# Separate semaphores for two groups of loads, an unrolled edge group, per-block waits in an expert's second layer, and first tokens over two queues

## The chip, the cores and the metric

The kernel runs on one core of one Trainium2 chip. The metric is the device time of one execution in microseconds; a profile of one further execution gives each engine's instructions with their times. Engines are named as in the profile: PE (TensorE; PEld is its weight load), DVE (VectorE), ACT (ScalarE), POOL (GpSimd), SP (SyncE, which here only issues transfers). SPq and ACTq are the sequencers of SP and ACT issuing transfers.

## The reference, cut to what matters

One layer on a graph of 3125 nodes (25 tiles of 128) with 256 features and 53125 edges sorted by `dst`:

```
xn = layernorm(x)
x  = x + gnn(xn, edges) + mix(xn)          # gnn: adjacency times features, two softmax layers; mix: linear attention
x  = x + moe(layernorm(x))                 # 8 experts, top 1, capacity 489 tokens
hmid = relu(einsum("ecd,edf->ecf", buf, w1) + b1)     # first layer of an expert, 256 -> 1024
ybuf = einsum("ecf,efd->ecd", hmid, w2) + b2          # second layer, 1024 -> 256
out  = x + gate * ybuf[token]
```

## The kernel before, in words

Each engine runs one instruction stream written out by hand; streams meet only at semaphores (`then_inc` raises one, `wait_ge` waits for a value), and an engine that waits holds everything behind it in its own stream.

**Start.** SP loads `dst`, DVE samples it, PE sums the samples, and DVE writes `base_i`: for each of the 25 tiles the place in the edge list at which its window begins. Meanwhile ACT issues the load of the first seven x tiles (`s_x[0]`) and of `wk`, `wv` (`s_kvw`), and then runs a small square root, with which the table of functions is loaded (L670). SP then runs over four groups of tiles, `GROUPS = ((0, 2), (2, 6), (6, 16), (16, 25))`. `window(g, j)` reads one number of `base_i` and issues three loads of 9 KB (`src`, `dst`, `edge_weight`), which raise `s_win[g]`. Group 0 is written out; the other three are loops on the sequencer (`sp.Fori`). After group 0 SP issues the rest of x (three loads and one short one, L454, L457) and the five weights `wo`, `wq`, `W0`, `W1`, `b1` (L461). After group 1 it issues eleven small constants (L451). The five and the eleven raise the same semaphore `s_w`, and whoever needs any of them waits for all 16.

**First stage, an iteration `it` for each tile.** ACT copies a turned tile (`turned`), casts a new group's windows (`cast(g)`, in the iteration before the group's first tile, L700 to L702), normalizes a tile, pairs (`paired`), squares (`squares`, after PE's `product`), and moves the records of the tile before out of PSUM (`kept`). DVE prepares a group (`prepare(g)`, L946 to L959), spreads a tile's edges (`spread`, L967, L969), takes statistics of x in `it < 3` and variances in `it == 2` and `scales(1)` in `it == 3`, slots the tile before (`slot(it - 1)`, L976, L979, L983) and, from `it == 2`, builds one-hot tiles (`hots`, L1023 to L1029). PE runs `product`, `ranks`, `slots` of the tile before, `build` from `it == 3` and the turn of the next tile. In `it == 1` it also runs `others()`, 15 transposes of `wo`, `W0`, `W1` and `b1` behind the wait for all of `s_w`; ACT moves them out in `others_out()`. POOL also waits for `s_w`, much later, after the attention matrix.

**Graph stages** (to about 947 us): adjacency blocks are built, applied and stored, then read back for two layers; this is not touched.

**Experts.** POOL scatters tokens into `xbuf_dram` (`s_disp`) and the rows to be kept into `rbuf_dram` (`s_dres`). PE runs `WARM` = 11 products of no use to cover the wait. SP issues `tokens(0, 0)` and `tokens(1, 1)`, four transfers of 128 KB each, then waits for `s_dres` and issues `kept_rows(0, 0)`, the output of x (`before(0, NT)`) and `kept_rows(1, 1)`. DVE transposes the tokens (`columns`, L1370), and for each expert PE runs

```
up(e):    8 blocks f, 2 matmuls each, into three PSUM banks           -> s_hid
ACT:      hidden(e): relu of block f into hmT[:, f, :]                -> s_hidv
down(e):  wait for s_hidv >= 8e + 8; 4 blocks of rows, each a sum over the 8 f   -> s_y
DVE:      yblock(e): 4 blocks of rows scaled and cleaned; POOL scatters them
```

A float32 matmul appears in the profile as two instructions.

Of the kernel before, what the change touches and what calls it, by code (L numbers as in the profile page):

```python
# [19 lines left out]
NT = 25  # L20
# [26 lines left out]
EPS = 1e-5  # L47
NWL = 16
XG = ((0, 7), (7, 13), (13, 19), (19, 25))
# [59 lines left out]
def graph_program(nc, a, out):  # L109
    ctx = ExitStack()  # L110
    with ctx:
# [227 lines left out]
        s_rstd = sem("s_rstd")  # L339
        s_w = sem("s_w")  # L340
        s_wt = sem("s_wt")
        s_wtc = sem("s_wtc")
# [83 lines left out]
        def _(sp):  # L426
# [10 lines left out]
            for g, (t0, t1) in enumerate(GROUPS):  # L437
                if g == 0:
                    for j in range(t0, t1):
                        window(g, j)  # L440
                else:
                    with sp.Fori(t0, t1) as j:
                        window(g, j)
                if g == 1:
                    for to, src in ((gate_w[:, :, :], half("L0_ffn_gate_w")), (bo_b[:, :], a["L0_mix_bo"].partition_broadcast(P)), (gb1_b[:, :], a["L0_gnn_b1"].partition_broadcast(P)),
                            (gate_b[:, :], a["L0_ffn_gate_b"].partition_broadcast(P)),
                            (gvb[:, 0, :], a["L0_mix_ln_v_g"].partition_broadcast(P)), (gvb[:, 1, :], a["L0_mix_ln_v_b"].partition_broadcast(P)),
                            (cols[:, 0:1], col("L0_gnn_b0")),
                            (cols[0:HD, 1:2], col("L0_mix_ln_k_g")), (cols[HD:P, 1:2], col("L0_mix_ln_k_g")),
                            (cols[0:HD, 2:3], col("L0_mix_ln_k_b")), (cols[HD:P, 2:3], col("L0_mix_ln_k_b"))):  # L450
                        sp.dma_start(to, src).then_inc(s_w, 16)  # L451
                for x in {0: (1, 2, 3)}.get(g, ()):
                    t0, last = XG[x][0], min(XG[x][1], NT - 1)
                    sp.dma_start(X1[:, t0:last, :], a["x"][t0 * P:last * P, :].rearrange("(j p) d -> p j d", p=P)).then_inc(s_x[x], 16)  # L454
                    if XG[x][1] == NT:
                        sp.wait_ge(s_zero, 1)
                        sp.dma_start(X1[0:LAST, last, :], a["x"][last * P:N, :]).then_inc(s_x[x], 16)  # L457
                if g == 0:
                    for to, src in ((wo_n, half("L0_mix_wo")), (wq_n, half("L0_mix_wq")), (W0_n, a["L0_gnn_W0"]),
                                    (W1_n, a["L0_gnn_W1"]), (b1_n, a["L0_ffn_b1"])):  # L460
                        sp.dma_start(to, src).then_inc(s_w, 16)  # L461
            sp.wait_ge(s_zero, 3)
# [48 lines left out]

            def tokens(e, s):
                blocks = xbuf_dram[ds(e * XS, XS), :].rearrange("(b j) (q f) -> q j b f", j=32, q=4)
                for q in range(4):
                    sp.dma_start(xbs[32 * q:32 * q + 32, s, :, :], blocks[q]).then_inc(s_tok[s], 16)
# [34 lines left out]
            sp.wait_ge(s_disp, 16 * NT)  # L550
            tokens(0, 0)
            tokens(1, 1)
            sp.wait_ge(s_dres, 16 * NT)
            kept_rows(0, 0)
            before(0, NT)
            kept_rows(1, 1)
# [107 lines left out]
        def _(act):  # L664
            half = lambda name: a[name].rearrange("(r p) n -> p r n", p=P)
            act.dma_start(X1[:, 0:XG[0][1], :], a["x"][0:XG[0][1] * P, :].rearrange("(j p) d -> p j d", p=P)).then_inc(s_x[0], 16)
            act.dma_start(wk_n, half("L0_mix_wk")).then_inc(s_kvw, 16)
            act.dma_start(wv_n, half("L0_mix_wv")).then_inc(s_kvw, 16)
            act.wait_ge(s_const, 2)
            nc.scalar.activation(rsum[:, 0, 0:1], ones_f[:, 0:1], ACT.Sqrt)  # L670
            act.wait_ge(s_const, 9)
# [87 lines left out]
            for it in range(NU + 3):  # L759
# [20 lines left out]
                if 0 <= u < NU:  # L780
                    evac(u)
                    if u - 1 in [strip_end(k) for k in range(NS)]:
                        strip_out(strip_of(u - 1))
                if it == 1:
                    others_out()
# [73 lines left out]
            def hidden(e):  # L859
                for f in range(8):  # L860
                    act.wait_ge(s_hid, 8 * e + f + 1)
                    if f == 0:
                        ge(act, s_y, 4 * e)
                    nc.scalar.activation(hmT[:, f, 0:CAPX], ps[:, 2 + f % 3, 0:CAPX], ACT.Relu, bias=b1T[:, f, e:e + 1]).then_inc(s_hidv, 1)  # L864
            for e in range(NE):
                hidden(e)
# [515 lines left out]
        def _(pe):  # L1382
# [15 lines left out]
            def others():  # L1398
                pe.wait_ge(s_w, 16 * NWL)
                for r in range(2):  # L1400
# [111 lines left out]
            for it in range(NU + 4):  # L1512
                if it < NT:
                    product(it)
                if it < NT:
                    ranks(it)
                if it == 1:
                    others()
# [204 lines left out]
            def down(e, s):  # L1723
                pe.wait_ge(s_hidv, 8 * e + 8)
                for c in range(4):
                    n = min(P, CAPX - c * P)
                    ge(pe, s_yv, 4 * e + c - 1)
                    o = ps[0:n, 5 + c % 2, 0:D]
                    for f in range(8):
                        last = nc.tensor.matmul(o, hmT[:, f, c * P:c * P + n], w2s[s][:, f, :], start=(f == 0), stop=(f == 7))  # L1730
                    last.then_inc(s_y, 1)
# [28 lines left out]
```

## Time and profile before

| what | us |
|---|---|
| median of 3 runs | 1199.76 |
| the runs | 1198.54 to 1200.06 |
| the profiled execution, its own time | 1197.42 |
| its span from first to last instruction | 1195.6 |
| PE busy | 1112.7 |
| DVE busy | 708.8 |
| ACT busy | 316.0 |
| mean granted TensorE clock | 0.976 of full speed |

The span is shorter than the time by 1.8 us that lie outside the instructions. A busy share is a mean over stages: PE is nearly always at work after the first 120 us, and far less before.

### The profile page before, as it was taken

How to read it: one execution, taken by the hardware profiler on the slowest of the kernel's cores; microseconds unless marked ns; L12 is line 12 of the kernel's file. 1: busy time of each engine (PE TensorE's matmuls, PEld its weight loads, DVE VectorE, ACT ScalarE, POOL GpSimd, SP SyncE). 2: the span in 40 equal slices, each digit the busy share in tenths (PEclk: the TensorE clock that was granted, in tenths of full speed). 3: DMA queues.
4: the chain of work that ended last, by engine and by line, in shares of the span. 5: the costliest groups of instructions: out<-in, count | busy, mean ns of one | idle time of the engine just before them, and what ended most of it. 6: DMA issues, size and time to landing. Idle time of an engine off the chain costs nothing.

```text
span 1195.6 us, 14060 instructions
## 1 busy us (share of the span) xinstructions
PE 1112.7 (93%) x4867; PEld 700.0 (59%) x4867; DVE 708.8 (59%) x1563; ACT 316.0 (26%) x1035; POOL 166.6 (14%) x206
## 2 busy tenths in 40 slices
PE   3589989999999999999998999999999699999995
PEld 2356656666666666666683444545558456666664
DVE  7798999998786877768740010204536334554443
ACT  3468767521212212112220111101112111222220
POOL 1013223301010100000000000000333511111111
PEclk9789989999999999999998999999999799999998
DMA  5111110122323333332238988787884564555510
GB/s 162 18 12 46 45 45 18 72 88 90 140 103 139 122 121 127 120 156 94 88 116 318 350 314 306 267 309 267 300 305 149 159 199 113 117 141 131 136 58 7
DMA packets 78724, 175.37 MB, mean 147 GB/s; under 512 B 33567, under 2 KB 62010, under 8 KB 66622
## 3 DMA queue, kind: packets, MB, share of 16 engines
q1 hardware_dynamic: 68462, 124.02, 32.8%
q10 hardware_dynamic: 6064, 42.40, 8.8%
q0 software_dynamic: 4128, 8.04, 1.9%
q8 instruction: 41, 0.67, 0.2%
q14 instruction: 29, 0.24, 0.1%
HBM read 113.82 MB, written 63.09 MB: 148 GB/s over the span
## 4 chain that ended last, share of the span: by engine, by line
PE 80%; DVE 9%; issue 3%; ACT 3%; another core or an unknown queue 2%; SPq 2%; DMA 1%; POOL 0%; POOLq 0%; DVEq 0%; ACTq 0%
PE ps L1481 20%; PE ps L1631 18%; PE ps L1464 11%; PE ps L1730 9%; PE ps L1719 9%; PE ps L1448 2%; PE ps L1507 2%; PE ps L1385 2%; PE ps L1434 2%; DVE W L983 1%; PE ps L1483 1%; PE ps L1733 1%; DVE RY L979 1%; ACT W L715 1%
## 5 line engine op out<-in xcount | busy, mean ns | idle before, releaser
L1481 PE MATMUL ps<-RING,XX 128*128 128x512 f32 x600 | 283.1, 594 | 0.3 <-ACT RING L743 0.3
L1631 PE MATMUL ps<-RING,RY 128*128 128x512 f32 (+2 forms) x750 | 277.5, 527 | 4.6 <-issue 4.6
L1631 PEld LDWEIGHTS ps<-RING,RY 128*128 128x128 f32 x750 | 134.0, 192 | 131.2 <-issue 129.1
L1464 PEld LDWEIGHTS ps<-RING 128*128 128x128 f32 x1250 | 163.7, 193 | 45.8 <-issue 44.7
L743 ACT COPY RING<-ps 128x512 f32<-128x512 f32 (+1 forms) x157 | 91.6, 584 | 317.0 <-PE ps L1464 300.7
L1464 PE MATMUL ps<-RING 128*128 128x128 f32 x1250 | 171.1, 278 | 0.5 <-ACT RING L733 0.5
L1481 PEld LDWEIGHTS ps<-RING,XX 128*128 128x128 f32 x600 | 102.9, 191 | 73.2 <-issue 72.0
L1023 DVE TENSOR_TENSOR RING<-iota_n,RY 128x512 f32<-128x512 f32 (+1 forms) x157 | 108.0, 688 | 43.6 <-PE ps L1464 38.9
L1029 DVE TENSOR_TENSOR RING<-iota_n,RY 128x512 f32<-128x512 f32 (+1 forms) x157 | 117.3, 747 | 0.0
L864 ACT ACTIVATE RY<-ps,b1T 128x489 f32<-128x489 f32 x64 | 42.8, 669 | 179.7 <-PE ps L1719 178.7
L1032 DVE TENSOR_TENSOR RING<-RING,RY 128x512 f32<-128x512 f32 x132 | 90.2, 683 | 0.0
L1358 DVE SCALAR_TENSOR_TENSOR W<-ps,RING,W 128x256 f32<-128x256 f32 (+1 forms) x32 | 15.5, 484 | 111.1 <-PE ps L1730 110.1
L636 POOL DMA_INDIRECT xbuf_dram<-XX,sidx x25 | 24.7, 989 | 345.1 <-DVE sidx L1298 339.6
L1202 DVE TENSOR_REDUCE nmx<-ps 128x4 f32<-128x512 f32 (+1 forms) x7 | 4.4, 634 | 113.9 <-PE ps L1385 113.9
L622 POOL TENSOR_TENSOR XX<-XX,bo_b 128x256 f32<-128x256 f32 x25 | 29.3, 1173 | 255.0 <-PE ps L1464 255.0
L1730 PE MATMUL ps<-RING,RY 128*128 128x256 f32 (+1 forms) x256 | 56.3, 381 | 3.0 <-ACT RY L864 3.0
L1730 PE MATMUL ps<-XT,RY 128*128 128x256 f32 (+1 forms) x256 | 56.3, 381 | 3.0 <-ACT RY L864 3.0
L659 POOL DMA_INDIRECT out<-W,RING x32 | 31.3, 978 | 198.0 <-DVE W L1365 181.3
L1730 PEld LDWEIGHTS ps<-RING,RY 128*128 128x128 f32 (+1 forms) x256 | 47.1, 185 | 13.8 <-ACT RY L864 6.2
L1730 PEld LDWEIGHTS ps<-XT,RY 128*128 128x128 f32 (+1 forms) x256 | 47.1, 185 | 13.7 <-ACT RY L864 6.2
L1719 PE MATMUL ps<-RING,XT 128*128 128x489 f32 x128 | 53.2, 574 | 1.5 <-issue 1.5
L1448 PE MATMUL ps<-wkvT,XT 128*128 128x512 f32 x100 | 50.9, 633 | 4.0 <-ACT XT L706 4.0
(251 smaller groups left out, 1268.3 us busy)
## 6 DMA issues: line engine op xcount, KB each, us to landing
RING<-adj_dram SPq DMA_DIRECT2D x62, 1280.0 KB
adj_dram<-RING ACTq DMA_DIRECT2D x31, 1280.0 KB, 4.6
rbuf_dram<-W SPq DMA_DIRECT2D x8, 516.0 KB, 5.5
RING<-rbuf_dram SPq DMA_DIRECT2D x8, 516.0 KB, 4.1
xbuf_dram<-W SPq DMA_DIRECT2D x8, 512.0 KB, 3.2
XT<-in_L_ffn_w SPq DMA_DIRECT2D x16, 256.0 KB
XT<-in_L_ffn_w SPq DMA_DIRECT2D x4, 1024.0 KB
RING<-in_L_ffn_w SPq DMA_DIRECT2D x16, 256.0 KB
```

The costliest lines, as they stand in the source:

```text
L659: gp.indirect_dma_start(out[:, :], bass.IndirectOffsetOnAxis(ap=rbs[0:n, e % 2, c, D + 1:RES].bitcast(I32), axis=0), ybs[0:n, e % 2, c, :] ...
L743: nc.scalar.copy(RING[:, n % 2, u % 5 * 512:u % 5 * 512 + w], ps[:, u % 2, 0:w]).then_inc(s_bev, 1)
L864: nc.scalar.activation(hmT[:, f, 0:CAPX], ps[:, 2 + f % 3, 0:CAPX], ACT.Relu, bias=b1T[:, f, e:e + 1]).then_inc(s_hidv, 1)
L1023: v.tensor_tensor(h[:, 0, 0:n, :], every, grid(0), ALU.is_equal).then_inc(s_eq, 1)
L1029: last = v.tensor_tensor(h[:, 1, 0:n, :], every, grid(1), ALU.is_equal)
L1032: last = v.tensor_tensor(h[:, 0, 0:n, :], h[:, 0, 0:n, :], grid(2), ALU.mult)
L1448: last = nc.tensor.matmul(ps[:, PROD, :], XT[:, c, m * P:(m + 1) * P], wkvT[:, c, :], start=(c == 0), stop=(c == 1))
L1464: last = nc.tensor.matmul(o[:, i * P:(i + 1) * P], h[:, 0, i, :], h[:, 1, i, :], start=True, stop=(j != s))
L1481: last = nc.tensor.matmul(ps[:, ACC + dd, :], w, at, start=(j == 0), stop=True, skip_group_check=True)
L1631: last = nc.tensor.matmul(o, (Y if l == 0 else S0)[:, j, :], RING[:, slot_of[g % 5], i * across + first:i * across + first + w], start=(j ...
L1719: last = nc.tensor.matmul(ps[:, 2 + f % 3, 0:CAPX], w1s[s][:, c, f * P:(f + 1) * P], xbT[:, s, c, 0:CAPX], start=(c == 0), stop=(c == 1))
L1730: last = nc.tensor.matmul(o, hmT[:, f, c * P:c * P + n], w2s[s][:, f, :], start=(f == 0), stop=(f == 7))
```

## The change

- The five weights wait on a semaphore of their own, `s_wt5`, and are issued after the windows of group 1, just ahead of the constants; `s_w` counts the eleven constants.
- `others()` waits for `s_wt5` alone and runs one iteration later (`it == 2`), and so does `others_out()`.
- The windows of group 1 are written out and not looped.
- ACT's small square root comes ahead of its three loads.
- ACT issues two of the four transfers of expert 0's tokens; SP issues the other two, and issues expert 1's tokens behind `kept_rows(0, 0)`.
- `down(e)` waits in its first block of rows for one hidden block at a time.

```diff
-NWL = 16
+NWL = 11
...
+        s_wt5 = sem("s_wt5")
...
             for g, (t0, t1) in enumerate(GROUPS):
-                if g == 0:
+                if g < 2:
                     for j in range(t0, t1):
                         window(g, j)
                 else:
                     with sp.Fori(t0, t1) as j:
                         window(g, j)
                 if g == 1:
+                    for to, src in ((wo_n, half("L0_mix_wo")), (wq_n, half("L0_mix_wq")), (W0_n, a["L0_gnn_W0"]),
+                                    (W1_n, a["L0_gnn_W1"]), (b1_n, a["L0_ffn_b1"])):
+                        sp.dma_start(to, src).then_inc(s_wt5, 16)
...
-                if g == 0:
-                    for to, src in ((wo_n, half("L0_mix_wo")), (wq_n, half("L0_mix_wq")), (W0_n, a["L0_gnn_W0"]),
-                                    (W1_n, a["L0_gnn_W1"]), (b1_n, a["L0_ffn_b1"])):
-                        sp.dma_start(to, src).then_inc(s_w, 16)
...
-            def tokens(e, s):
+            def tokens(e, s, quarters=(0, 1, 2, 3)):
...
-                for q in range(4):
+                for q in quarters:
...
             sp.wait_ge(s_disp, 16 * NT)
-            tokens(0, 0)
-            tokens(1, 1)
+            tokens(0, 0, (0, 1))
             sp.wait_ge(s_dres, 16 * NT)
             kept_rows(0, 0)
+            tokens(1, 1)
             before(0, NT)
...
+            act.wait_ge(s_const, 2)
+            nc.scalar.activation(rsum[:, 0, 0:1], ones_f[:, 0:1], ACT.Sqrt)
             act.dma_start(X1[:, 0:XG[0][1], :], a["x"][0:XG[0][1] * P, :].rearrange("(j p) d -> p j d", p=P)).then_inc(s_x[0], 16)
             act.dma_start(wk_n, half("L0_mix_wk")).then_inc(s_kvw, 16)
             act.dma_start(wv_n, half("L0_mix_wv")).then_inc(s_kvw, 16)
-            act.wait_ge(s_const, 2)
-            nc.scalar.activation(rsum[:, 0, 0:1], ones_f[:, 0:1], ACT.Sqrt)
...
-                if it == 1:
+                if it == 2:
                     others_out()
...
+            act.wait_ge(s_disp, 16 * NT)
+            for q in (2, 3):
+                act.dma_start(xbs[32 * q:32 * q + 32, 0, :, :], xbuf_dram[0:XS, :].rearrange("(b j) (q f) -> q j b f", j=32, q=4)[q]).then_inc(s_tok[0], 16)
             for e in range(NE):
                 hidden(e)
...
             def others():
-                pe.wait_ge(s_w, 16 * NWL)
+                pe.wait_ge(s_wt5, 16 * 5)
...
-                if it == 1:
+                if it == 2:
                     others()
...
             def down(e, s):
-                pe.wait_ge(s_hidv, 8 * e + 8)
                 for c in range(4):
...
                     for f in range(8):
+                        if c == 0:
+                            pe.wait_ge(s_hidv, 8 * e + f + 1)
                         last = nc.tensor.matmul(o, hmT[:, f, c * P:c * P + n], w2s[s][:, f, :], start=(f == 0), stop=(f == 7))
```

## Rows read from the trace of the kernel before

**Rows 1.** The page: shares of the chain that ended last, by engine.

```profile
PE 80%; DVE 9%; issue 3%; ACT 3%; another core or an unknown queue 2%; SPq 2%; DMA 1%; POOL 0%; POOLq 0%; DVEq 0%; ACTq 0%
```

**Rows 2.** PE's waits: releaser: us in total, times, longest.

```profile
PE ps L1385 <- DMA cols<-in_L_mix_ln_k_b: 12.5, 1, 12.5
...
PE ps L1730 <- ACT RY L864: 6.1, 8, 0.8
```

**Rows 3.** Timeline, first 18 us: start, duration, engine, line, [idle before it <-releaser].

```profile
2.41 1.28 ACT L670 ACT_TABLE_LOAD   x1 [2.41 <-issue]
...
6.16 0.18 DVE L907 CAST W<-W 125x17 f32<-125x17 int32 x1 [1.93 <-DMA W<-in_dst]
...
9.41 0.41 SPq L436 DMA_DIRECT2D HB<-in_src  x1
...
11.52 0.34 SPq L436 DMA_DIRECT2D HB<-in_src  x1
...
15.92 2.33 SPq L461 DMA_DIRECT2D RING<-in_L_mix_wo  x1
```

**Rows 4.** Transfers from 3.0 to 3.5 us, SP's queue: packets, MB, share of 16 engines.

```profile
q1 hardware_dynamic: 34, 0.06, 30.5%
```

**Rows 5.** Timeline of SP's queue, group 1, constants, start of group 2.

```profile
21.63 0.36 SPq L436 DMA_DIRECT2D HB<-in_src  x1
...
24.23 0.35 SPq L436 DMA_DIRECT2D HB<-in_src  x1
...
35.51 1.24 SPq L451 DMA_DIRECT2D cols<-in_L_mix_ln_k_b  x2
...
37.70 0.37 SPq L436 DMA_DIRECT2D HB<-in_src  x1
```

**Rows 6.** Timeline of DVE, iterations 1 to 5.

```profile
26.94 1.37 DVE L983 TENSOR_TENSOR W<-HB 128x2340 bf16<-128x2340 bf16 x1
...
32.82 0.20 DVE L946 TENSOR_SCALAR W<-HB 128x72 f32<-128x72 f32 x1 [4.51 <-ACT HB L702]
...
45.08 0.69 DVE L1023 TENSOR_TENSOR RING<-iota_n,RY 128x512 f32<-128x512 f32 x1 [1.56 <-POOL RY L605]
...
51.69 0.27 DVE L893 RECIPROCAL lna<-lnr 128x18 f32<-128x18 f32 x1 [3.39 <-ACT lnr L689]
...
53.12 0.64 DVE L976 TENSOR_REDUCE HB<-ps 128x18 f16<-128x468 f32 x1
...
69.15 0.40 DVE L995 RECIPROCAL hta<-hrs 128x40 f32<-128x40 f32 x1
```

**Rows 7.** Timeline of ACT and SP's queue: casts of groups 1 and 2, last window of 2.

```profile
32.16 0.25 ACT L700 CAST HB<-HB 128x72 f32<-128x72 int32 x1 [8.04 <-DMA HB<-in_edge_weight]
...
65.38 0.34 SPq L436 DMA_DIRECT2D HB<-in_edge_weight  x1
...
67.27 0.33 ACT L700 CAST HB<-HB 128x180 f32<-128x180 int32 x1
```

**Rows 8.** Stretches: us, busy time by engine, PEclk, DMA share, GB/s.

```profile
27.00:39.00 12.00, 0.00 (x0) 0.00 (x0) 7.20 (x24) 3.68 (x22) 0.00 (x0) 0.70 0.23 29
...
80.00:85.00 5.00, 3.58 (x26) 3.58 (x27) 4.96 (x8) 1.18 (x11) 0.99 (x3) 0.50 0.11 12
85.00:90.00 5.00, 5.00 (x18) 3.12 (x18) 4.97 (x7) 3.04 (x8) 0.62 (x1) 0.85 0.12 10
```

**Rows 9.** Timeline of PE, expert 0.

```profile
959.70 13.36 PE L1719 MATMUL ps<-RING,XT 128*128 128x489 f32 x32 [1.54 <-issue]
973.82 14.08 PE L1730 MATMUL ps<-XT,RY 128*128 128x256 f32 x64 [0.76 <-ACT RY L864]
```

**Rows 10.** Timeline of SP's queue and DVE around the first tokens.

```profile
953.55 4.32 SPq L515 DMA_DIRECT2D RING<-xbuf_dram  x8
...
958.84 1.30 DVE L1370 STREAM_TRANSPOSE RING<-RING 128x512 f32<-128x512 f32 x2 [10.28 <-DMA RING<-xbuf_dram]
...
977.65 0.48 DVE L1358 SCALAR_TENSOR_TENSOR W<-ps,RING,W 128x256 f32<-128x256 f32 x1 [10.29 <-PE ps L1730]
```

## The prediction

> **What bounds the kernel now.** I read the page first. The chain that ended last is on PE for 80% of the span [rows 1], so time is saved where PE stands idle, or early, where PE itself is fed by others. PE's waits show two such places that this change touches: one wait of 12.5 us for the last small constant (the last of the 16 transfers that `others()` waits for), and eight waits of 6.1 us together for ACT's last hidden block, one for each expert [rows 2]. Then the timelines of the first 70 us, by engine, to see what is next in line when the first wait is gone [rows 3, 5 to 7], the granted clock there [rows 8], and the timelines around the experts [rows 9, 10].
>
> What the reader is to see in the early rows: while PE waited, ACT waited too, 8.04 us for the windows of group 1 [rows 7], and DVE waited 4.51 us for ACT's casts of them [rows 6]. So PE's 12.5 us are no gain by themselves: SP's queue is behind all three waits. It is a chain of issues, one after the other, and it goes on to group 2.
>
> **Part 1, SP's queue.** How far does it move ahead? Three terms.
> - `dst` lands earlier, because ACT now runs its table load of 1.28 us [rows 3] and its square root ahead of its loads of x, `wk`, `wv`, which so far ran beside `dst`. DVE waited 1.93 us for `dst` [rows 3] and everything else it needs was there, so the gain is between 0 and 1.9. During the load SP's queue held at most 30.5% of the 16 engines' time, which is 5 of 16 [rows 4]: part of the duration is its own. I take 1.0.
> - Group 1 is written out. A looped window takes 24.23 - 21.63 = 2.60 us [rows 5], a written-out one 11.52 - 9.41 = 2.11 [rows 3]. Three periods give 1.5, and the loop's start some 0.3 (from the last constant's end, 36.75, to the first `src` at 37.70 are 0.95 us [rows 5], which holds the reading of `base_i` too): 1.8.
> - The issue of `wo` took 2.33 us [rows 3] against 0.41 for a window's, held up behind 2.3 MB of x in the queue. The weights now come 8.5 us later (four windows at 2.11), so this hold is gone, or else falls on the first window. Between 0 and 1.9; I take 0.8.
>
> The five weights and eleven constants stay ahead of group 2, so they cost it what they cost now. Group 2 starts earlier by 1.0 + 1.8 + 0.8 = 3.6 us, with ends at 1.8 and 5.6. On the other side, x, `wk` and `wv` are issued up to 1.9 us later (behind the table load); the five engines that carried `dst` are free then, so I take 0.3 as the delay of the first normalized tile, bounds 0 and 1.9.
>
> A rule of the Trainium skill bears on `dst` (DMA: Bandwidth & Descriptors, "Why a DMA increments its semaphore by 16 and not by 1"): a transfer uses as many engines as divide its slowest dimension, here 5 for 125 partitions. The 30.5% of [rows 4] agrees. By that page's 27 GiB/s an engine, its 42 KB an engine take an estimated 1.5 us alone, which puts the first term nearer 1.9, and the sum would be 11.4 in place of 10.5.
>
> **Part 2, what the first stage could do with its waits gone.** Group 1 now lands by about 26 us (SP's x loads end near 14.9, the four windows 8.4 later, the hold 1.0, landing under 2), which is before DVE has finished slot 0 at 26.94 + 1.37 = 28.31 [rows 6]. ACT's and DVE's waits go. `others()` in `it == 2` needs weights issued by about 27; PE gets there at about 37 (slots 0 from 28.6, a turn that waits for ACT, `product(2)` and `ranks(2)` stand ahead). It then lies under DVE's slot 1, which ends near 39: hidden, at 2.7 us (15 products at 0.18). Without that cover it would cost these 2.7. What DVE does from 28.31 on is its own work: 32.82 to 43.52 (45.08 less 1.56 idle), 10.7; then 45.08 to 48.30, 3.2; then, the wait of 3.39 gone because ACT's root comes earlier by more, 51.69 to 53.12, 1.4 [rows 6]. So slot 2 starts at 28.31 + 0.3 + 15.3 = 43.9 instead of 53.12: 9.2 us.
>
> That gain does not survive iteration 5. There ACT casts group 2. Before, its last window was issued at 65.38 and the cast ran at 67.27 without idle [rows 7]: just in time. Now the cast could run at 67.27 - 9.2 = 58.1, but the window comes 3.6 earlier only, and the cast at 63.7. ACT waits some 5.6 us in order, behind it the square root for DVE's `head_scale` (L995, only 1.9 us behind the cast before [rows 6, 7]), and `kept(4)`, for which PE's turn waits. So all three are late together, and the first stage keeps **3.6 us**. The last group is cast ten iterations after group 2, which leaves its loads time enough; later stages follow PE's work alone and carry the 3.6 to the end.
>
> The clock: it went from 2.4 to 1.2 GHz in PE's idle stretch from 27 to 39 (mean 0.70) and again was low in 80 to 86.5 [rows 8]. The new wait gives PE another gap of some 4 us, the old one is gone. A low stretch as in [rows 8] has 3.58 + 1.5 = 5.1 us of PE work, half of which, 2.5 us, is lost. One such stretch more or less is as likely: 0 in the sum, 2.5 either way in the range.
>
> **Part 3, `down`.** Block 0 of the hidden activations is done long before the first product needs it. The seven products ahead of the last take two instructions of 14.08 / 64 = 0.22 each [rows 9]: 3.1 us, while ACT needs 0.76 for its last block. The gap closes: 8 x 0.76 = **6.1 us** [rows 2]. Added are 7 waits an expert. `up` waits in the same way for every block and has 13.36 / 32 = 0.42 us for 489 columns at 2.4 GHz (0.41 if nothing is lost), so a passed wait costs under 0.02: at most 1.1 us for 56, I take 0. The next in line is DVE's `yblock`; its first product came after 10.29 us of idleness [rows 10], so it doesn't bind.
>
> **Part 4, tokens.** Eight issues took 4.32 us, 0.54 each; DVE got the first tokens at 958.84 [rows 10] and PE idled 1.54 us between the last warm product and `up(0)` [rows 9], which bounds the gain. Two issues saved are 1.1, if the 16 engines keep up, with POOL's scatter in flight; 0 if they don't. I take **0.8**. A rule of the Trainium skill (DMA: Bandwidth & Descriptors, "Issuing engines are not separate DMA queues") says that a second queue saves only the sequencer's time; by it the term would be the whole 1.1 where nothing else binds. Expert 1's tokens now wait for POOL's last five scatters too, some 7 us, and DVE's transposes of them stand ahead of `yblock(0)`: done near 970, wanted at 977.65 [rows 10], so 0; more than 7 us of further lateness would be needed. ACT's two issues lie in its idle time before `hidden(0)`. The output of x comes 2 us later, under expert 0.
>
> **Sum.** 3.6 + 6.1 + 0.8 = 10.5 us. The profiled execution took 1197.42 (span 1195.6 and 1.8 around it); it becomes 1186.9. The median of the runs is 2.3 higher, and so I predict 1199.76 - 10.5 = **1189.3**.
>
> **Rivals.**
> - *SP's queue moves further.* Group 2's ten windows took 65.38 - 37.70 = 27.7 us [rows 5, 7], at group 1's period they would take 24.5. With `dst` and the hold at their better ends the start gains up to 5.6 + 3.2 = 8.8, with 7 as its middle: 13.9 in all, 1185.9. For it: 9.2 are there to be taken. Against: the change doesn't touch this loop. Chance 0.20.
> - *SP's queue moves by the unrolling alone,* 1.8: 8.7 in all, 1191.1. For it: the hold may simply fall on the first window, and `dst` uses 5 engines either way. Chance 0.22.
> - *The gap before `down` is not closed,* because waits ahead of each product keep PE from loading weights ahead: 10.5 - 6.1 = 4.4, 1195.4. Against it are `up`'s waits. Chance 0.08.
> - *One low-clock stretch more:* 1191.8. Chance 0.09.
> - *Slower.* With its gaps near 28, 38 and 60 us PE stays at 1.2 GHz from 40 us up to 90. PE is at work some four fifths of that at full clock, so it would need about 20 us more: 1199.8 + 9.5 = 1209. It turns the sign from about 26 us of low-clock PE work on. Against it: the low stretch after 80 ended once PE was fully busy [rows 8], and a PE at 1.2 GHz is busy. Chance 0.03.
> - The forecast has the rest, 0.38.
>
> **Range.** The first two rivals and one clock stretch stretch it from 1183.5 (start 7 to 8.8, tokens 1.5) to 1194.5 (start 1.8, tokens 0, one stretch more, waits at 1.1). About 0.2 is left out: the unclosed gap, the slow case, and the tails. 0.2% of this time is 2.4 us, about what a measurement here can tell from no change. Every case but the slow one is over that, save a corner of the unclosed gap together with a small first term: faster 0.94, within 0.2% 0.03, slower 0.03.
>
> **What would show it.** In the profile after: PE's wait for a constant is gone; ACT waits before its cast of group 2 (not 1) for a transfer, 4 to 7 us; the first window is issued near 8.4, group 2's first near 34; `up(0)` starts 3.6 + 0.8 = 4.4 us earlier, near 955.3; PE's waits for ACT before L1730's group are gone. The prediction is wrong if ACT does not wait for group 2 (then the start gives more), if `up` to `down` still has 0.7 us of idleness, or if PE's granted clock is low over 40 to 60 us.

## The result and the profile after

| | before | after |
|---|---|---|
| median of the runs, us | 1199.15 (4 runs) | 1182.02 (4 runs, 1180.75 to 1184.12) |
| ratio after / before | | 0.986, 95% interval 0.9842 to 0.9877 |
| profiled execution, us (span) | 1197.42 (1195.6) | 1184.12 (1182.3) |
| mean granted clock | 0.976 | 0.975 |

The change gains 17 us (14.7 to 18.9 by the interval) where 10.5 were forecast, and ends 1.5 us below the range. The two profiled executions differ by 13.3 us only; the one of after happens to be the slowest of its four, and the part on TensorE's stop below says where such differences come from.

In the line numbers of after, the window's transfers are L437, the weights L448, the constants L455, the casts L700 as before, DVE's first steps on a group L949, the slot's start L979, `up` L1722 and `down` L1734.

Timeline of SP's queue in the kernel after, the `src` issue of the windows named in the text, the first weight and the last constants:

```profile
8.41 0.41 SPq L437 DMA_DIRECT2D HB<-in_src  x1
...
15.76 1.40 SPq L437 DMA_DIRECT2D HB<-in_src  x1
18.83 0.34 SPq L437 DMA_DIRECT2D HB<-in_src  x1
20.86 0.35 SPq L437 DMA_DIRECT2D HB<-in_src  x1
22.88 0.34 SPq L437 DMA_DIRECT2D HB<-in_src  x1
24.23 0.43 SPq L448 DMA_DIRECT2D RING<-in_L_mix_wo  x1
...
32.57 1.24 SPq L455 DMA_DIRECT2D cols<-in_L_mix_ln_k_b  x2
35.05 0.37 SPq L437 DMA_DIRECT2D HB<-in_src  x1
...
55.85 0.35 SPq L437 DMA_DIRECT2D HB<-in_src  x1
58.37 0.35 SPq L437 DMA_DIRECT2D HB<-in_src  x1
```

Timeline of DVE, ACT and PE in the same trace: the read of `dst`, slot 2's start, ACT's cast of group 2, a DVE step that follows it, DVE's first step on group 2, and expert 0:

```profile
5.11 0.23 DVE L910 CAST W<-W 125x17 f32<-125x17 int32 x1 [0.88 <-DMA W<-in_dst]
...
42.97 0.64 DVE L979 TENSOR_REDUCE HB<-ps 128x18 f16<-128x468 f32 x1
...
61.05 0.34 ACT L700 CAST HB<-HB 128x180 f32<-128x180 int32 x1 [2.51 <-DMA HB<-in_edge_weight]
62.55 0.40 DVE L998 RECIPROCAL hta<-hrs 128x40 f32<-128x40 f32 x1 [1.73 <-ACT hrs L772]
66.44 0.24 DVE L949 TENSOR_SCALAR W<-HB 128x180 f32<-128x180 f32 x1
...
954.66 13.36 PE L1722 MATMUL ps<-RING,XT 128*128 128x489 f32 x32 [0.76 <-issue]
967.85 13.98 PE L1734 MATMUL ps<-XT,RY 128*128 128x256 f32 x64
981.67 1.80 PE L1722 MATMUL ps<-RING 128*128 128x489 f32 x4
```

The reader is to see four things. PE's wait for a constant is gone (it is in no row of PE's waits). `dst` comes 1.05 us earlier [rows 3], but group 2's first window only 2.65 us (37.70 to 35.05 [rows 5]). Group 2's last window is issued at 58.37 where it was 64.26 in the kernel before, 5.9 us earlier: the loop itself became faster, 2.53 us a window for 2.79. ACT waits for it as forecast, but 2.51 us and not 5.6 (2.5 to 3.9 us in all traces with this start). And `down` starts 13.19 us after `up(0)` (954.66) instead of 14.12 [rows 9], with no wait for ACT.

For the start I use one marker from here on: DVE's first step on group 2 (L946 of before, L949 of after), which all later stages follow. It stood at 73.02 and stands at 66.44.

### The profile page after: what moved, and what is told of

Its sections match the earlier page's. It is cut to its first block, busy times and chain, and to the rows that moved or that the text cites. A ratio compares the mean times of both kernels' runs of the same rounds, so it can differ in the third digit from the quotient of the medians.

```text
span 1182.3 us, 14039 instructions
## 1 busy us (share of the span) xinstructions
PE 1115.0 (94%) x4867; PEld 703.8 (60%) x4867; DVE 708.6 (60%) x1563; ACT 316.7 (27%) x1035; POOL 167.8 (14%) x206
## 4 chain that ended last, share of the span: by engine, by line
PE 83%; DVE 6%; issue 4%; SPq 4%; ACT 2%; another core or an unknown queue 1%; DMA 0%; POOL 0%; POOLq 0%; DVEq 0%; ACTq 0%
PE ps L1634 21%; PE ps L1484 20%; PE ps L1467 11%; PE ps L1734 9%; PE ps L1722 9%; PE ps L1510 2%; SPq L437 2%; PE ps L1451 2%; PE ps L1388 1%; PE ps L1437 1%; PE ps L1486 1%; PE ps L1737 1%; DVE W L986 1%; PE ps L1670 1%
## 5 line engine op out<-in xcount | busy, mean ns | idle before, releaser
L1634 PE MATMUL ps<-RING,RY 128*128 128x512 f32 (+2 forms) x750 | 280.5, 532 | 4.6 <-issue 4.6
L1634 PEld LDWEIGHTS ps<-RING,RY 128*128 128x128 f32 x750 | 137.0, 197 | 131.2 <-issue 129.0
L1361 DVE SCALAR_TENSOR_TENSOR W<-ps,RING,W 128x256 f32<-128x256 f32 (+1 forms) x32 | 15.5, 484 | 98.8 <-PE ps L1734 97.8
L1734 PE MATMUL ps<-RING,RY 128*128 128x256 f32 (+1 forms) x256 | 55.9, 379 | 0.0
L1734 PE MATMUL ps<-XT,RY 128*128 128x256 f32 (+1 forms) x256 | 55.9, 379 | 0.0
L1722 PE MATMUL ps<-RING,XT 128*128 128x489 f32 x128 | 53.2, 574 | 0.8 <-issue 0.8
L1722 PE MATMUL ps<-RING 128*128 128x489 f32 x128 | 53.1, 573 | 0.0
L1734 PEld LDWEIGHTS ps<-XT,RY 128*128 128x128 f32 (+1 forms) x256 | 47.4, 185 | 9.3 <-issue 1.8
```

The source lines that it names most:

```text
L1634: last = nc.tensor.matmul(o, (Y if l == 0 else S0)[:, j, :], RING[:, slot_of[g % 5], i * across + first:i * across + first + w], start=(j ...
L1722: last = nc.tensor.matmul(ps[:, 2 + f % 3, 0:CAPX], w1s[s][:, c, f * P:(f + 1) * P], xbT[:, s, c, 0:CAPX], start=(c == 0), stop=(c == 1))
```

## The experiments

Kernels of one group below ran on one chip, together with the kernel before, and each ratio is against that. The kernel before had medians of 1189.2, 1198.8, 1198.6 and 1200.1 us in the four groups; why the first is lower is told under TensorE's stop. The expectations count the start as 7.45 us, about the shift at the first matmul of the layers (634.07 to 626.59, 7.48); the marker gives 6.58, and the last part says why it is the steadier measure. The times that they name for group one are counted from a kernel before at 1199 us, and it ran at 1189.2 there, so in that group only differences can be compared.

### Group one: the parts alone, and the loops

`e1_down_only`, the kernel before and

```diff
-                pe.wait_ge(s_hidv, 8 * e + 8)
...
                     for f in range(8):
+                        if c == 0:
+                            pe.wait_ge(s_hidv, 8 * e + f + 1)
```

> The kernel before, with the waits of the second layer's first block taken one by one and nothing else changed. Theory 1 (the gap was wider than the recorded idle time of 0.76 us in front of the layer): the period from one expert to the next falls by about 1.03 us, as between the two traces, and the time by 8.3 us (8 x 1.03), to about 1191. Rival (0.76 us an expert, the rest of the 17 us belongs to the start): the time falls by 6.1 us, to about 1193. Start and tokens stay where they were: first matmul of expert 0 at 959.7 +- 3 in the trace, the ACT cast of group 2 at 67.3.

Measured: 1180.93 us, ratio 0.9933 (0.9920 to 0.9946), so -8.0 us (-6.4 to -9.5). The period from one expert's `up` to the next is 27.01 us (950.83 to 977.84). Theory 1 holds; 6.1 lies outside the interval, if only just.

`e2_start_only`, the changed kernel with that edit reversed, and the tokens too:

```diff
-            tokens(0, 0, (0, 1))
+            tokens(0, 0)
+            tokens(1, 1)
             sp.wait_ge(s_dres, 16 * NT)
             kept_rows(0, 0)
-            tokens(1, 1)
```

(and ACT's two transfers of the tokens taken out).

> The changed kernel with the second layer's single wait and the four SP token transfers put back: only the edits of the start are left. Theory 1 (the start gives 7.45 us, of which 3.3 come from the loop of edge group 2 that runs at 2.53 us a window instead of 2.79): time falls by 7.5 us, to about 1191.7, and the last window of group 2 is issued near 59.4. Rival (the start gives only the 3.6 us of the queue's moves, and something later gave the rest): time falls by 3.6 us, to about 1195.6. The period per expert stays 27.96 us and the first matmul after the columns is as in the kernel before.

Measured: 1181.57 us, 0.9933 (0.9921 to 0.9945), so -8.0 us (-6.5 to -9.4). The marker is at 66.49, group 2's last `src` at 58.12, and the period is 28.03 us (943.68 to 971.71). The start gives what the trace of after shows. 3.6 is outside.

`e3_group1_looped`, the changed kernel with `if g < 1:` for `if g < 2:`.

> The changed kernel with edge group 1 issued by a loop again. Theory 1 (where the loop of group 2 lies in SP's program decides its period): the four windows of group 1 cost 1.8 to 2.1 us more (4 x 0.5), and group 2's loop goes back to about 2.79 us a window (10 x 0.26 more), so the ACT cast of group 2 comes 4.4 to 4.7 us later and the time is 1186.5. Rival (the period of group 2's loop follows from what else moves data at that time, or from the written-out group only through its own cost): group 2 stays at 2.53 us a window, the cast comes 1.8 to 2.1 us later, the time is 1184.

Measured: 1175.69 us, 0.9891 (0.9877 to 0.9906), so -13.0 us. Its marker stands at 70.16, 3.7 us behind after's. Timeline of SP's queue of this kernel, two issues of group 1, three of group 2 and three of group 3:

```profile
19.26 0.35 SPq L437 DMA_DIRECT2D HB<-in_src  x1
21.81 0.34 SPq L437 DMA_DIRECT2D HB<-in_src  x1
...
53.70 0.35 SPq L437 DMA_DIRECT2D HB<-in_src  x1
56.48 0.36 SPq L437 DMA_DIRECT2D HB<-in_src  x1
59.27 0.35 SPq L437 DMA_DIRECT2D HB<-in_src  x1
...
69.86 0.36 SPq L437 DMA_DIRECT2D HB<-in_src  x1
72.41 0.36 SPq L437 DMA_DIRECT2D HB<-in_src  x1
74.96 0.36 SPq L437 DMA_DIRECT2D HB<-in_src  x1
```

One and the same loop body takes 2.55, 2.79 and 2.55 us for groups 1, 2 and 3, as in the kernel before, and group 2's is the slow one as soon as group 1 is a loop too. Theory 1 (the period changes) holds against the rival; of the 4.4 to 4.7 us expected for the cast 3.7 were seen (64.77 for 61.05). The time is 13.0 us below the kernel before, some 4 less than the changed kernel's gain, as the marker says.

`e5_before_pad4`, four waits on a semaphore that is long reached, ahead of group 2's loop:

```diff
+                if g == 2:
+                    for _ in range(4):
+                        sp.wait_ge(s_base, 1)
```

> The kernel before, with four waits on a semaphore that has long been reached put into SP's program just ahead of the loop of edge group 2: they cost a few tenths of a us at most and move the loop's code by four instructions. Theory 1 (place of the code in memory sets the period): the period of group 2's loop changes from 2.79 us, towards 2.53, and that of group 3's loop may change too; at 2.53 the cast of group 2 starts about 2.5 us earlier and the time falls by 2 to 3 us. Rival (the traffic or the time in the kernel sets it): the period stays 2.79 and the time stays within 0.5 us of before.

### Group two: the same loop at another place

`e6_before_pad36`, 36 such waits ahead of group 2's loop, whose body then begins at the 90th instruction, exactly where group 3's began.

> The kernel before, with 36 reached waits ahead of the loop of group 2: they move its code to exactly the offset in SP's program at which the loop of group 3 stands in the kernel before (which runs at 2.55 us a window), at a cost of about 1.4 us. Theory 1 (the offset sets the period): group 2's loop falls from 2.79 to 2.55 us a window, 2.4 us in all, and the time is about 1 us below before. Rival (the second of three loops is slow wherever it lies, or the traffic of that time makes it slow): the period stays 2.79 and the time is 1 to 1.4 us above before.

`e7_before_pad58_group1`, 58 ahead of group 1's loop, which puts its body on the 72nd instruction, where group 2's was.

> The kernel before, with 58 reached waits ahead of the loop of group 1: its code then stands at exactly the offset at which the slow loop of group 2 stands in the kernel before. Theory 1 (the offset sets the period): group 1's loop takes 2.79 us a window instead of 2.55 and group 2's 2.55 instead of 2.79. Rival (order or time sets it): group 1 stays at 2.55 and group 2 at 2.79. The time itself is a few us above before, from the waits, and says nothing.

Measured: 1199.00 us for the first, 1.0003 (0.9988 to 1.0018); 1202.32 for the single run of the second. SP's queue of `e6_before_pad36`, group 2:

```profile
38.81 0.36 SPq L436 DMA_DIRECT2D HB<-in_src  x1
41.41 0.34 SPq L436 DMA_DIRECT2D HB<-in_src  x1
43.95 0.35 SPq L436 DMA_DIRECT2D HB<-in_src  x1
46.48 0.35 SPq L436 DMA_DIRECT2D HB<-in_src  x1
```

and of `e7_before_pad58_group1`, three issues of group 1 and three of group 2:

```profile
26.75 0.35 SPq L436 DMA_DIRECT2D HB<-in_src  x1
29.56 0.35 SPq L436 DMA_DIRECT2D HB<-in_src  x1
32.34 0.35 SPq L436 DMA_DIRECT2D HB<-in_src  x1
...
43.49 0.35 SPq L436 DMA_DIRECT2D HB<-in_src  x1
46.03 0.35 SPq L436 DMA_DIRECT2D HB<-in_src  x1
48.56 0.35 SPq L436 DMA_DIRECT2D HB<-in_src  x1
```

The slowness went with the place, in both directions. The loops, by the instruction of SP's compiled program, counted from 0, at which the body (14 instructions, the same but for the semaphore) begins. The periods are means without a group's first turn, which is often longer, and without turns that hold one long issue:

| body begins at | kernels | us a window |
|---|---|---|
| 38, 43 | group 1 of e3, e13; of before, e6 | 2.53 to 2.54 |
| 72 | group 2 of before, e3, e13; group 1 of e7 | 2.79 to 2.80 |
| 74 | group 2 of e5 | 2.78 |
| 90, 92, 94 | groups 2 and 3 of several; group 2 of after | 2.53 to 2.55 |
| 101 to 119 | groups 2 and 3 of e7, group 3 of after, e6 | 2.53 |
| 194 | group 3 of e4, e14 (below) | 2.56 |

So order and traffic are out, the place is shown. What at the 72nd to 87th instruction costs a loop 0.26 us a turn isn't known. The Trainium skill (Runtime: NRT & Kernel Launch, "Instruction fetch mechanics") has instructions fetched in blocks of 256 and a cost for branches that leave the two blocks held; by that rule all these loops, within the first 208 instructions, would be alike, and the measurement says otherwise.

`e6_before_pad36` tells one thing more. Its group 2 starts 1.1 us later than in the kernel before (38.81 for 37.70, the cost of the waits) but its last window comes 1.7 us earlier (62.58 for 64.26), and yet the marker moved by 0.3 us only, to 72.70, and `dst` alone was read 0.4 us earlier there (5.72 for 6.16). It wasn't group 2's windows that held the kernel before.

`after_again`, the changed kernel itself.

> The changed kernel itself, unchanged, on the same chip as the others of this call. Theory (start 7.45 us, tokens 0.7, layers 8.3 us add up, and the kernel before is 10 us faster on a chip whose trace lacks the stop of TensorE near 933 us): 16.4 us below the kernel before of the same chip. Rival (part of the gain seen at first came from the stop near 933 us and the low clock behind it, and is gone where there is no stop): 13 us or less.

Measured: 1182.32 us, 0.986 (0.9838 to 0.9882), so -16.8 us; marker at 66.37.

`e4_group2_written`, `if g < 3:` for `if g < 2:`.

> The changed kernel with edge group 2 written out as well (ten windows, each 2.03 us instead of 2.53). Theory 1 (the ACT cast of group 2 waits for that group's last window, now 2.5 us): the last window comes 5 us earlier, ACT's wait is gone, and the time falls by the 2.5 us that ACT waited. Rival (by then another chain, ACT and DVE's own work before the cast, sets the time, or the earlier windows collide with other transfers): under 1 us.

Measured: 1182.09 us, 0.9855 (0.9831 to 0.9878). ACT's cast of group 2, in this kernel:

```profile
57.38 0.33 ACT L700 CAST HB<-HB 128x180 f32<-128x180 int32 x1
```

ACT's wait is gone and the marker is 2.8 us earlier (63.54), as theory 1 says, but not the 2.5 us in the time: it is the same as after_again's, as the rival has it. See the last group.

### Group three: the small terms

`e8_tokens_undone` has the token part of `e2_start_only`'s edit alone. `e9_sqrt_behind` puts ACT's square root back behind its loads. `e10_one_early_wait` waits twice an expert instead of eight times:

```diff
-                        if c == 0:
-                            pe.wait_ge(s_hidv, 8 * e + f + 1)
+                        if c == 0 and f in (0, 7):
+                            pe.wait_ge(s_hidv, 8 * e + (7 if f == 0 else 8))
```

`e11_all_written` writes out group 3 as well as group 2.

> The changed kernel with expert 0's tokens fetched by four SP transfers again, and expert 1's ahead of the rows kept for expert 0. Theory (the two queues give 0.7 to 0.8 us, two issues of some 0.5 us less in front of the first expert and two pieces landing together): the idle time of TensorE before the first expert's matmul goes from 0.8 to about 1.5 us, the time rises by 0.7. Rival (nothing, since another transfer lands last): both stay.

> The changed kernel with ACT's first square root, and the table load of 1.28 us that goes with it, behind its three loads again. Theory (the sample of dst that starts DVE landed 1.05 us earlier because ACT's loads left 0.4 us later and DVE and SP's first steps came forward with it): DVE's first instruction on dst goes back from about 5.1 to 6.2 us; the start of the layers comes up to 1 us later, and the time rises by as much, if group 2's windows set the start. Rival (the shift is hidden behind the x loads that SP issues from about 12 us): under 0.3 us.

> The changed kernel with two waits in front of each expert's second layer instead of eight: on the seventh block at its start, on the eighth before the last step of its first group. Theory (only the last block's ReLU, which ends 0.8 us after its matmuls, was ever late; eight waits instead of one cost nothing and bring nothing more): the period per expert stays 26.94 to 27.0 us. Rival (the gain of 1.03 instead of 0.76 us comes from waits on the earlier blocks, which let weight loads start sooner): the period rises by some 0.2 us and the time by up to 2 us.

> The changed kernel with groups 2 and 3 written out as well. Theory 1 (ACT's wait for group 2's last window is gone, as in the run that writes out group 2 alone: layers start 3 us earlier; group 3 has slack and gives nothing more): DVE's product for group 2 near 63.5, the first matmul of the layers near 623.4, and the time 3 us below the changed kernel unless the stop of TensorE near 920 takes it back: then the layers' last matmul group shows it. Rival (group 3's windows had become the next to be late, since its loop stayed behind): another 1 us or more off the start of the layers.

| kernel | median | ratio, interval | in its trace |
|---|---|---|---|
| e8 | 1181.47 | 0.9861 (0.9845 to 0.9876) | from the first warm product to `up(0)` 12.77 us |
| e9 | 1181.14 | 0.9857 (0.9838 to 0.9877) | `dst` read at 5.56, marker 65.83 |
| e10 | 1182.80 | 0.9869 (0.9854 to 0.9884) | 27.01 us an expert |
| e11 | 1182.11 | 0.9853 (0.9839 to 0.9867) | ACT's cast of group 2 at 57.49 without a wait, first matmul of the layers at 624.65 |

None differs from the changed kernel by what can be measured, so traces must tell. Tokens: from the first warm product to `up(0)` the nine kernels that fetch them by one queue take 12.6 to 13.1 us, the nine with two queues 12.0 to 12.4. The term is real, some 0.7, and the idle time meant by the expectation (1.5 us) was not there in e8 (0.27), since the warm products themselves ran longer. Square root: with the loads first, `dst` was read at 5.56 here and at 5.72 to 6.23 in the seven other traces with that order (mean of the eight 5.96), with the table load first at 4.98 to 5.36 in ten (mean 5.16). So the edit is worth some 0.8 us at `dst`, of the 1.05 seen in the first pair; at the marker nothing was lost without it (65.83 for 66.44). The rival holds for this edit as undone in the changed kernel. Waits: only the last block's mattered, and 48 waits more or fewer cost nothing that shows. Group 3: no sign of a further gain; the predicted 623.4 was missed by 1.3, which is within the scatter of that row.

### Group four: how the start's parts add up

`e12_before_group1_written` is the kernel before with `if g < 2:` for `if g == 0:`. `e13_order_only` is the kernel before with weights on their own semaphore behind group 1 and the transposes in `it == 2`:

```diff
+                if g == 1:
+                    for to, src in ((wo_n, half("L0_mix_wo")), ...
+                        sp.dma_start(to, src).then_inc(s_wt5, 16)
...
-                if it == 1:
+                if it == 2:
                     others()
...
-                pe.wait_ge(s_w, 16 * NWL)
+                pe.wait_ge(s_wt5, 16 * 5)
```

> The kernel before with one edit, edge group 1 written out. Theory 1 (two limits: TensorE's transposes of the weights wait for the last constant, and ACT's cast waits for group 2's windows; the kernel before is held by the first): the constants come 1.6 to 1.8 us earlier and all that waits for them too; group 2's loop runs at 2.53 us a window because its code now stands elsewhere, but its windows were not the last wait, so this gives nothing: 1.8 us in all. Rival (the loop's period is worth its whole 2.5 us by itself): 4 us or more.

> The kernel before with only the order edits of the start: weights behind group 1 and on a semaphore of their own, transposes after it == 2; group 1 stays a loop, ACT's square root stays behind its loads, tokens and second layer as before. Theory 1: TensorE and DVE are free of the constants (slot 2 near 43 instead of 53), but group 2's loop stands at the slow place (2.79 us a window) and its windows set the time: the ACT cast of group 2 comes near 65 with a wait of 6 to 7 us, the time falls by 2 to 2.9 us. Rival (the order edits are worth most of the 7.45 us by themselves): 5 us or more.

Measured: 1196.98 us, 0.998 (0.9968 to 0.9992), and 1195.28 us, 0.9964 (0.9949 to 0.9980). The markers are at 71.74 and 71.08. PE's waits of the first, 15 to 70 us (us in total, times, longest):

```profile
PE ps L1385 <- DMA cols<-in_L_mix_ln_k_b: 11.0, 1, 11.0
```

and ACT's cast of group 2 in the second:

```profile
65.69 0.34 ACT L700 CAST HB<-HB 128x180 f32<-128x180 int32 x1 [6.43 <-DMA HB<-in_edge_weight]
```

The first is still held by the constants (PE stands 11.0 us) though its loop runs at 2.53; the second is free of them and held by the slow loop (ACT stands 6.43 us). At the marker they give 1.3 and 1.9 us, 3.2 together, against 6.6 for the changed kernel. The times fell by 2.4 (1.0 to 3.8) and 4.3 us (2.4 to 6.1), with the scatter told below in them. Both theories 1 hold by the marker and the waits; the time of the second, and its first matmul of the layers (629.72, 4.35 us earlier), don't separate the 2.9 of the theory from the 5 of its rival. The changed kernel has the square root ahead as well, but this isn't what makes 6.6 of 3.2: without it (e9) the marker stood 7.2 us earlier than in the kernel before. How the 1.9 divides between the semaphore, the later weights and the later transposes no run shows.

`e14_group2_written_again` and `e15_changed_kernel_again` repeat two kernels side by side.

> The changed kernel with group 2 written out, a second time. Theory (the 3.1 us by which the layers start earlier are real, and were lost in the first timing to a longer stop of TensorE near 920 and the low clock behind it): on a chip whose traces lack this stop, 3 us below the changed kernel of the same call; on one with it, within 1.5 us of it, and the loss between the start of the layers and the first expert again 2 to 5 us more than in the changed kernel. Rival (something in the layers, not the stop, undoes the gain): no gain without the stop either.

> The changed kernel, for comparison in the same call. Theory: 16.4 us below the kernel before on the same chip, and in the trace, if it has the stop of TensorE near 920 to 930, some 8 to 11 us more between the start of the layers and the first expert than the traces without it (317.5).

Measured: 1181.81 us, 0.9844 (0.9823 to 0.9865), and 1182.59 us, 0.986 (0.9839 to 0.9880). Markers 65.17 and 66.18. Both traces have the stop. The theory's test, a chip without it, didn't come about; and the changed kernel lost more here between layers and experts (330.0 us) than the other (328.2), against what was expected. Whether writing out group 2 is worth its 1 to 2.8 us at the marker stays open: it is less than these runs can tell.

## Why the prediction was wrong, point by point

The sign, the places and the waits were as forecast. Two terms of the sum were too small, one of them for a reason that the prediction had named and turned down: that group 2's loop could run faster.

- **SP's queue up to group 2** (forecast 3.6, measured 2.65). `dst` 1.05 in this pair, as taken (0.8 in the mean of all traces, e9). Unrolling 1.5 (the four `src` issues of group 1 span 7.68 us in the kernel before and 6.09 in e12; the first window of group 2 there is 1.46 us earlier), so the three periods are right and the extra 0.3 for the loop's start isn't there. The hold (0.8 taken) did fall on the first window, 1.40 us at 15.76, instead of vanishing, as the second rival had it.
- **Group 2's loop: the step that failed.** "Against: the change doesn't touch this loop" holds for its code and not for its place in the program. Its ten windows took 5.9 - 2.65 = 3.2 us less: 2.6 by the shorter turns (0.57 in the first, 0.26 or so in each of the other eight), shown by e3, e6 and e7 to go with the place, and 0.6 because the one long issue happened to be shorter. So the cast came 6.2 us earlier and not 3.6. The rival "SP's queue moves further" had nearly the right start (7) from three sources; the loop's period was one of them and came true, the better ends of `dst` and of the hold did not. At the first matmul of the layers the start shows 7.5.
- **What the first stage could do.** Slot 2 started at 42.97, 10.15 us earlier (9.2 forecast). The cap by ACT's cast is shown three times at the marker: the wait is 2.51 us in after, 6.82 with the slow loop (e3), and gone when group 2 is written out (e4). That the gain needs both limits lifted is shown by e6 (the fast loop alone, nearly nothing), e12 and e13.
- **`down`, mis-sized term.** 0.76 us an expert was taken from the idle time ahead of L1730 [rows 9]; it was 1.02 (28.03 to 27.01), 8.0 us by e1 alone. The rows of before had it: `up`'s 32 matmuls are recorded with 13.36 us, but the recorded end of a matmul lies beyond the start of the next one that needn't wait. `down(0)` began at 973.82 and lasted 14.08, to 987.90 [rows 9], and `up(1)`, in the kernel before, had begun by then:

```profile
987.73 2.62 PE L1719 MATMUL ps<-RING 128*128 128x489 f32 x6
```

This 0.17 is to be added to the idle time, and so the gap was 0.93 (14.12 to 13.19 from `up` to `down`). The remaining 0.09 lies between `down` and the next `up` (13.91 to 13.82), where nothing was changed but the first block's waits; why it went isn't shown. Waits ahead of each product cost nothing that shows (e10). The prediction's bound for them, 0.02 us, was too low by its own numbers: `up` passes one wait for every four instructions, which makes 0.04 and 2.2 us in all.
- **Tokens**: 0.8 forecast, 0.67 between the two traces (`up(0)` 5.04 us earlier, the warm products 4.37). No cost from expert 1's tokens: `yblock(0)` began 3.74 us after `down(0)` (971.59), 3.83 before.
- **The clock** cost nothing that shows in the first stage: both traces have half speed from 39 to some 48 us and again in short stretches between 65 and 90, and full speed over 50 to 60. Where it did cost time, behind the stop told below, the prediction had no term.
- **The sum**, with the start taken at the marker, is 6.6 + 0.7 + 8.2 = 15.5 us, within the interval of the measured 17; the other 1.6 us belong to no term. The lower end of the range was missed although it held more for the start (8.8) and the tokens (1.5) than came: it left `down` at 6.1. At the upper end the listed terms add up to 1195.5 and not 1194.5.

**TensorE's stop, and why executions differ.** In the last product group of the layers, between 917 and 944 us, PE stands still for 4 to 5.7 us in every trace of the first pair, of groups two, three and four, and in none of group one. In the kernel before (timeline, ACT, DVE and SP's queue, which all wait for PE):

```profile
932.08 0.17 PE L1684 MATMUL ps<-wkvT,ones_b 128*128 128x16 bf16 x1
...
937.92 0.58 ACT L817 COPY XT<-ps 128x512 f32<-128x512 f32 x1 [6.84 <-remote]
937.93 0.17 DVE L1294 TENSOR_TENSOR wkvT<-ps,last_e 128x16 f32<-128x16 f32 x1 [4.61 <-remote]
937.99 0.80 SPq L509 DMA_DIRECT2D RING<-in_L_ffn_w  x2
...
938.73 0.58 PE L1647 MATMUL ps<-W1T,W 128*128 128x128 f32 x1 [5.32 <-ACT W L795]
```

DVE's step at 937.93 needs the matmul recorded at 932.08, and ACT and SP go on in the same tenth of a microsecond; the view names no releaser on this core (`remote`). So it is PE that was held, or its signals to the others; the trace doesn't say which. In seven of the nine traces of changed kernels with a stop it falls earlier, at another of these products. Half speed follows it. Windows of the kernel after (us, busy time and count of PE, weight loads, DVE, ACT, POOL, granted clock, DMA):

```profile
919.00:924.00 5.00, 0.90 (x6) 0.71 (x5) 0.46 (x2) 0.96 (x2) 3.78 (x5) 0.80 0.15 54
924.00:932.00 8.00, 8.00 (x40) 8.00 (x39) 2.75 (x12) 1.51 (x6) 3.73 (x4) 0.50 0.16 56
```

and of e3, in group one, around the same part of the program, where PE does 71 matmuls in 8 us for the 40 above:

```profile
907.00:919.00 12.00, 12.00 (x74) 10.82 (x74) 9.33 (x45) 2.48 (x8) 8.39 (x9) 1.00 0.58 197
919.00:927.00 8.00, 7.64 (x71) 7.41 (x69) 5.76 (x25) 2.41 (x9) 6.04 (x7) 1.00 0.26 84
```

From the first matmul of the layers to `up(0)` traces without the stop take 317.4 to 318.6 us, those with it 325.6 to 331.0. The difference, some 8 us in the profiled execution of the kernel before, accounts for most of the 10 us between its medians. In the first pair before took 325.6 and after 328.1, which is 2.5 of the 3.8 us by which the two profiled executions differ less than the medians. It is in both kernels and not part of the gain (e1 to e3 gained theirs without it); if anything the changed kernels lose more by it (326.1 to 331.0, before and its variants 325.6 to 327.0). What stops PE stays open. The chip isn't it as far as the record tells: groups one and three both ran on the chip numbered 0. Another scatter, of 2.3 us among three traces of the same kernel, lies between the marker and the layers (after 560.2, after_again 560.2, e15 557.9 us; before 561.1), so the shift of 7.5 at the layers is less sure than the 6.6 at the marker. e2's time alone gives 8.0 (6.5 to 9.4): what the start is worth between 6.6 and 8 stays open.

## What to carry to other kernels

When a wait is removed from a chain of limits, look for the next limit and ask what else the edit moves: here the order edits were worth 1.9 us, the written-out group 1.3, and all edits of the start together 6.6, since one had lifted the queue and the other the engines. Count a layer's gap from start to start of its groups, not by the idle time in front of a matmul, which misses the overlap of recorded ends (1.02 for 0.76 us). And a loop that only issues transfers is worth reading turn by turn for each place in which it stands: written out it takes 2.03 us a window instead of 2.53 to 2.80.

## What was not expected of the hardware

- A loop's period on SP depends on where its code lies: 2.79 to 2.80 us with its body at the 72nd instruction, 2.53 to 2.56 at the 38th, 43rd and from the 90th to the 194th, shown by moving it both ways.
- The stop of PE of 4 to 5.7 us between 917 and 944 us, followed by the clock at 1.2 GHz, in every trace of the first pair and of groups two to four and in none of group one; 8 to 13 us in all, its cause open.
- In most loops one issue takes 0.8 us or more instead of 0.34 (67.00, 1.35 us, in after), at another turn in each execution, and in written-out groups too (40.15, 0.83 us, in e11).
